# VectorE's product of B and u moved between the two scans of a tile, in a Mamba and expert layer on one core

## The reference

```python
x = x + mamba(layernorm(x))      # with its own rmsnorm and residual inside
x = x + experts(layernorm(x))    # 8 experts, each for its own 512 tokens

# in mamba, for 512 channels d and 16 states n:
xs  = silu(causal_conv4(xn @ W_in[:, :512]) + conv_b);  res = xn @ W_in[:, 512:]
dt, B, C = split(xs @ W_x);      dt = softplus(dt @ W_dt);  A = -exp(A_log)
h[t] = exp(A * dt[t]) * h[t-1] + dt[t] * B[t] * xs[t]      # per d and n, over all tokens
y[t] = sum over n of h[t] * C[t]
out  = residual + (y * silu(res)) @ W_out

# an expert:  (silu(x @ w1) * (x @ w3)) @ w2
```

## Time and profile before

| | us |
|---|---|
| median of 3 runs | 1081.07 (1079.33 to 1081.79) |
| the profiled execution | 1081.22 |
| its span, first to last instruction | 1079.4 |
| VectorE busy | 951.1 (88%) |
| TensorE busy | 948.8 (88%) |
| GpSimd busy | 892.4 (83%) |
| ScalarE busy | 679.7 (63%) |
| mean granted TensorE clock | 0.954 |

### The profile page before, as it was taken

One profiled execution on the slowest core, in us unless ns is written; L12 is line 12 of the kernel. 1 busy time (PEld: TensorE's weight loads), 2 busy tenths in 40 slices (PEclk: granted clock), 3 DMA queues, 4 the chain that ended last, 5 costly groups with the idle time before them and its releaser, 6 DMA issues.

```text
span 1079.4 us, 12931 instructions
## 1 busy us (share of the span) xinstructions
PE 948.8 (88%) x4128; PEld 597.4 (55%) x4128; DVE 951.1 (88%) x1039; ACT 679.7 (63%) x1147; POOL 892.4 (83%) x491
## 2 busy tenths in 40 slices
PE   5989678989999989989999899989999897768879
PEld 4445344655665556645656556645666455655655
DVE  5678698999998999998999999988999989998941
ACT  4455666676657766676667767677666765667410
POOL 1569689988998989988998979988998979998810
PEclk9899899999999999999999999999999999769889
DMA  4570118011651029010651028110560026200010
GB/s 160 240 272 1 59 42 311 1 62 49 224 198 39 23 93 366 12 61 18 237 216 40 22 94 320 58 62 0 209 261 16 27 93 257 82 20 21 34 46 20
DMA packets 42852, 117.86 MB, mean 109 GB/s; under 512 B 8608, under 2 KB 27040, under 8 KB 32672
## 3 DMA queue, kind: packets, MB, share of 16 engines
q1 hardware_dynamic: 40928, 116.99, 29.2%
q10 hardware_dynamic: 1856, 0.04, 0.1%
HBM read 110.21 MB, written 6.82 MB: 108 GB/s over the span
## 4 chain that ended last, share of the span: by engine, by line
DVE 28%; issue 18%; PE 17%; ACT 11%; POOL 11%; DVEq 0%; POOLq 0%; ACTq 0%
DVE ring L657 18%; PE gbank L997 11%; DVE ring L642 7%; POOL hc L506 6%; POOL ring L492 4%; PE ybank L1043 3%; ACT ebank L783 3%; ACT hb L937 1%; ACT sres L847 1%; ACT xin L921 1%; ACT xs L843 1%; DVE dt_ L622 1%; ACT x L890 1%; PE gbank L1104 1%; ACT L848 1%
## 5 line engine op out<-in xcount | busy, mean ns | idle before, releaser
L506 POOL TENSOR_TENSOR hc<-ring,c_all 128x1024 f32<-128x1024 f32 x255 | 599.6, 2369 | 108.6 <-DVE ring L657 87.1
L657 DVE TENSOR_TENSOR_SCAN ring<-ebank,state,ring 128x512 f32<-128x512 f32 x512 | 624.0, 1267 | 61.8 <-ACT ebank L783 54.9
L783 ACT ACTIVATE ebank<-dt_,a_neg 128x512 f32<-128x512 f32 x512 | 349.1, 688 | 260.7 <-DVE ring L657 258.9
L1043 PE MATMUL ybank<-ident,hc 128*128 128x128 f32 x2048 | 274.7, 282 | 76.6 <-ACT yt L863 55.1
L1043 PEld LDWEIGHTS ybank<-ident,hc 128*128 128x128 f32 x2048 | 242.5, 146 | 173.4 <-issue 75.0
L492 POOL TENSOR_TENSOR ring<-b_all,u 128x1024 f32<-128x1024 f32 x95 | 225.1, 2369 | 0.0
L642 DVE TENSOR_TENSOR ring<-b_all,ubank 128x1024 f32<-128x1024 f32 x159 | 189.9, 1195 | 0.0
L997 PE MATMUL gbank<-xT,w 128*128 128x512 f32 x320 | 156.4, 628 | 28.2 <-ACT xT L802 15.7
L997 PE MATMUL gbank<-xT,w_a 128*128 128x512 f32 x256 | 119.2, 610 | 5.5 <-DVE dt_ L622 3.2
L997 PEld LDWEIGHTS gbank<-xT,w 128*128 128x128 f32 x320 | 59.7, 199 | 90.9 <-issue 75.6
L997 PE MATMUL gbank<-xs,w_a 128*128 128x512 f32 x224 | 104.0, 608 | 0.0
(11 more groups left out here) (127 smaller groups left out, 748.2 us busy)
## 6 DMA issues: line engine op xcount, KB each, us to landing
b_all<-bc_kept SPq DMA_DIRECT2D x32, 1024.0 KB, 7.0
c_all<-bc_kept SPq DMA_DIRECT2D x32, 1024.0 KB, 8.2
w<-in_L_ffn_w_dram SPq DMA_DIRECT2D x16, 640.0 KB, 4.9
w_a<-wc_kept SPq DMA_DIRECT2D x7, 1024.0 KB, 4.8
w_a<-win_kept SPq DMA_DIRECT2D x6, 1024.0 KB, 6.3
w2s<-in_L_ffn_w_dram SPq DMA_DIRECT2D x8, 640.0 KB, 4.5
xin<-in_L_attn_x_dram SPq DMA_DIRECT2D x9, 512.0 KB, 3.6
x<-in_L_attn_x_dram SPq DMA_DIRECT2D x7, 512.0 KB, 6.4
```

Of the source, the lines that this page charges most:

```text
L506: ch_ok.by(e.tensor_tensor(hc[:, q % HC, :, :], ring[:, q % RING, :, :], c_all[:, n:n + NG, :], ALU.mult))
L657: h_ok.by(e.tensor_tensor_scan(row, ebank[j % 2][:, :], row, initial=state[:, q, n:n + 1], op0=ALU.mult, op1=ALU.add))
L783: e_ok.by(e.activation(ebank[j % 2][:, :], dt_[:, d, :], ACT.Exp, scale=a_neg[:, d, k:k + 1]))
L1043: last = e.matmul(ybank[:, cols(b)], hc[:, q % HC, n, cols(b)], ident[:, :], is_transpose=True, start=(k == 0 and n == 0 and b == 0), stop ...
```

## The change

In VectorE's group of a tile the product for the next tile is issued behind the first scan instead of behind the second. The condition on which tile gets a product is the same.

```diff
                     row = ring[:, q % RING, n, :]
                     h_ok.by(e.tensor_tensor_scan(row, ebank[j % 2][:, :], row, initial=state[:, q, n:n + 1],
                                                  op0=ALU.mult, op1=ALU.add))
-                if q + 1 < Q and q + 1 in DVE_BU:
-                    bu(c, q + 1)
-                elif q + 1 == Q and has_scan(c + 1):
-                    bu(c + 1, 0)
+                    if n == 0 and q + 1 < Q and q + 1 in DVE_BU:
+                        bu(c, q + 1)
+                    elif n == 0 and q + 1 == Q and has_scan(c + 1):
+                        bu(c + 1, 0)
```

## The result

The changed kernel takes 1106.03 us (median of 4 runs, 1104.16 to 1109.92) against 1081.38 (4 runs, 1079.33 to 1081.79): 1.0237 times as long, 95% interval 1.0202 to 1.0271, so 24.7 us slower. Runs of one kernel differ in steps (25 runs of before on another chip lie at 1074.3 to 1075.1, 1076.9 to 1077.4, 1079.2 to 1079.8 and 1081.2 to 1082.4), so medians one or two us apart say little by themselves. The profiled execution took 1107.74 us, its span is 1105.9, 26.5 more than before.

What follows compares the result with a forecast made beforehand. VectorE was taken as the bound between set-up and tail, its time growing with a few long waits. 6.7 + 6.9 + 6.0 + 7.4 - 0.3 = 26.7 us on 1081 gave 1108 us, range 1097 to 1115 for 8 in 10.

Steps and rivals of the forecast that it cites:

- the chains: Unbroken runs of ScalarE work between exponentials, each starting as a tile's second scan ends, with VectorE waiting behind.
- A: Wait ahead of tile 9, behind ScalarE's state copy, table loads and silus: 1.11 us later in chunks 1 to 6, 6.7 us.
- 7 b: Second of tile 7's two scans (a is the first, b the second); forecast to end 1.11 us later.
- B: Wait ahead of tile 13, behind ScalarE's state, two copies and four normalisations: about 1 us in chunks 1 to 7, 6.9 us.
- D: Wait ahead of tile 29, behind GpSimd's unbroken work from tile 22: 1.1 us in chunks 0 to 5, together 7.4 us.
- the softplus wait at tile 27: VectorE's new 1.1 us wait ahead of tile 27; inside tile 29's delay in chunks 0 to 5, alone in chunk 6.
- C: Stretch to tile 21, through u copy, softplus and gated silu: 0.1 to 2.3 us a chunk by chunk, together 6.0 us.
- the u bank: Product for tile 16 waits for ScalarE's copy of u into its bank: a new wait of 0.3 us.
- The step that was left open: VectorE's step from a product to the tile's second scan: taken as 1.11 us; 1.23 at all 159 would add 19 us.
- The faster rival: ScalarE's long chains hang on something other than the second scan, so only savings stay: 1072 us, 6 in 100.
- The half rival: Idle ScalarE and GpSimd catch up on the stretches to tiles 21 and 29: 1089 us, 8 in 100.
- The one for more: Product to second scan takes 1.23 us and TensorE's clock falls once more per chunk: 1124 us, 6 in 100.

Runs made afterwards that it cites:

- the fillers above: Four matmuls that nobody reads added ahead of the expert's first ones in chunks 1 to 7, against the kernel before: 1082.72 us against 1079.68, ratio 1.0032.

## Why the prediction was right

The forecast was 1108 us; the profiled execution took 1107.74, the median of the runs is 1106.03. The sign and the mechanism were right: five moves at the starts of the chains bring the whole loss, thirteen others none that the median shows, and an operation of half the length in the same place costs half.

A held in its mechanism: the wait is 3.28 (3.3 foretold) and tile 9 starts 8.78 behind the end of 7 b. In size it is 1.1 us too low, nearly all of it since tile 7 itself comes 0.11 to 0.18 later behind tile 0. The prediction let a wait at tile 3 take up the time saved from 29 to 0, and there is one:

```profile
441.17 1.28 DVE L657 TENSOR_TENSOR_SCAN ring<-ebank,state,ring 128x512 f32<-128x512 f32 x1 [0.18 <-ACT ebank L783]
```

In the table the saving stands in the row 29 to 0 (-0.13 where nothing else moved) and the new wait in A. B held to 0.1 us, D to 0.2; in D the softplus wait at tile 27 lay inside, as said.

C was mis-sized, 4.4 against 6.0, and lies below the prediction's own bounds too (4.6 to 7.6 by its terms, where it writes 4.7 to 7.5). Of its chain, the wait ahead of tile 17 (1.02, 1.1 foretold) and the gated silus' 7.36 came out; the u bank cost 0.19 instead of 0.3 (492.41 less 489.85 is 2.56, where two scans and the way to a product are 2.37). The step that failed is that TensorE loses its clock at the turned x as before, only later, and tile 21 so comes at 32.65 in chunks 3 to 6. The turned x does come later, as foretold: 9.91 behind 13 a (492.31 + 1.06 - 483.46; 9.92 foretold). But TensorE kept its clock. ScalarE's copy and TensorE in chunk 3 of after:

```profile
492.31 1.06 ACT L802 ACTIVATE xT<-gbank 128x512 f32<-128x512 f32 x2
```

```profile
493.63 3.67 PE L997 MATMUL gbank<-xT,w 128*128 128x512 f32 x8 [1.81 <-ACT xT L802]
```

It waited 1.81 instead of 2.92, and its eight records took 3.67 instead of 5.37, so the chain's own 32.15 (32.19 foretold) stood alone, 0.07 above before. In chunks 1 and 2 that same chain costs 1.77.

That the sum came out so near was luck. The 1.1 that A has more and the 1.6 that C has less nearly cancel. The prediction put the stretch from 29 to 0 at nothing. After shows two waits for a residual sum there, and ahead of each, eight of TensorE's matmul records ran in part at 1.2 GHz, at a granted clock of 0.62 and 0.71. VectorE's two waits and those records:

```profile
808.22 0.69 DVE L676 TENSOR_TENSOR x<-x,gbank 128x512 f32<-128x512 f32 x1 [1.97 <-PE gbank L997]
```

```profile
935.21 0.69 DVE L676 TENSOR_TENSOR x<-x,gbank 128x512 f32<-128x512 f32 x1 [1.11 <-PE gbank L997]
```

```profile
794.52 5.75 PE L997 MATMUL gbank<-xs,w_a 128*128 128x512 f32 x8
...
922.21 5.06 PE L997 MATMUL gbank<-xs,w_a 128*128 128x512 f32 x8
```

At full clock eight records of this size take 3.60 (the fillers above), so 2.15 and 1.46 went there. Before had one wait of that kind, ahead of chunk 2:

```profile
296.62 0.69 DVE L676 TENSOR_TENSOR x<-x,gbank 128x512 f32<-128x512 f32 x1 [1.17 <-PE gbank L997]
```

These, the -2.09 in chunk 7 and the +1.0 at the end nearly cancel. None of them was foretold.

The step that was left open, product to second scan, is 1.11. The Trainium skill, VectorE: DVE Perf Modes, section "The DRAIN you can't avoid", says that the next operation waits for an empty pipe; it adds that an operation which is not held starts earlier, which the prediction leaves out. The trace fits the addition: the scan that doesn't read the product starts 1.11 behind it, while the product lasts 1.20. The section also says that a semaphore between two operations costs nothing extra; here the scan that reads the product, and waits for its semaphore, starts 1.23 behind it, 0.12 later. But the 0.12s that this saves did not come back as time: VectorE's busy time fell by 2.8 us, and of the stretches only that from 29 to 0 shows them, 0.13 each.

The faster rival fell because the chains do start at the end of scan b (460.77 and 460.81). The half rival needed ScalarE and GpSimd to catch up, and they only waited longer. The one for more, at 1124, fell with the 1.11; of its other half, TensorE's clock, the trace shows the two waits ahead of chunks 6 and 7 on VectorE's path.

## What to carry to other kernels

Where an engine in order feeds others through two banks in turn, moving independent work in front of an operation is free only if nobody who ends a later wait starts at that operation's end: find the waits, walk each back to the instruction that starts its chain, and count only moves ahead of these. The same list tells where to win: taking 1 us out of one such chain brought 11 to 12.5 us here, about half of it by TensorE's clock as the traces have it. A wait that covers another one hides its price until it is removed, so price a move again on every new base.

## What the runs showed of the hardware

TensorE's clock changed where other engines shifted by a microsecond. The same eight matmul records take 3.67 us at a granted clock of 1.00 and 5.37 at 0.68, behind idle times of 0.97 and 2.92; which chunks are hit differed from kernel to kernel, and with several chunks at 1.7 us each it moved the sum by more than some of the edits. The idle time ahead does not decide alone: behind 3.37 and 3.36 us of it, the same four records took 3.62 us in one chunk and 1.88 in another. Where such a place lies on the chain, the stretches of the trace tell more than the median.
